# Inverse roots of the queries' and keys' mean squares by GpSimd, projections earlier in the order, in the first stage of a two-layer transformer kernel

## The reference

```
def _rmsnorm(x, scale):
    ms = jnp.mean(jnp.square(x), axis=-1, keepdims=True)
    return x * jax.lax.rsqrt(ms + EPS) * scale
...
h = _layernorm(x) * (1 + ca) + sa
q = (xh @ wq + bq).reshape(b, s, 16, 16)
k = (xh @ wk + bk).reshape(b, s, 4, 16)
v = (xh @ wv + bv).reshape(b, s, 4, 16)
q = _rmsnorm(q, q_norm_scale)
k = _rmsnorm(k, k_norm_scale)
q, k = rope(q) * head_scale, rope(k)
probs = softmax(causal(q k^T * head_scale))
x = x + ga * (probs v @ wo + bo)
h = _layernorm(x) * (1 + cb) + sb
x = x + gb * ffn(h)
```

## Time and profile before

| | |
|---|---|
| median of 3 runs | 1146.43 us (1146.34 to 1146.93) |
| profiled execution | 1145.18 us, of which the span of instructions is 1143.5 us |
| mean granted TensorE clock | 0.970 |
| first stage | from 0 to about 241 us of the span |
| later stages | attention of the second layer to about 965 us, then the experts |

### The profile page before, as it was taken

The page is one execution under the profiler, slowest core; times in us unless marked ns, Lnnn a source line. Parts: engine busy times, 40 slices in busy tenths (PEclk is TensorE's granted clock), DMA queues, the critical chain, the costliest instruction groups (busy, mean ns, idle before and its releaser), DMA issues. The chain is left out here.

```text
span 1143.5 us, 22333 instructions
## 1 busy us (share of the span) xinstructions
PE 1060.2 (93%) x7536; PEld 923.7 (81%) x7536; DVE 895.2 (78%) x1817; ACT 736.2 (64%) x1399; POOL 334.6 (29%) x335
## 2 busy tenths in 40 slices
PE   5888888879999999999999999999999997979996
PEld 4656666658899899899898898898998986769994
DVE  5788988857788788788788788788788787867775
ACT  4679797767766666666666666666666654625661
POOL 3353544442311201211111111111111234753440
PEclk9889999979999999999999999999999998989999
DMA  7210001010401311311311211221221291824436
GB/s 256 94 52 16 16 6 44 14 50 23 137 21 50 112 47 47 108 45 52 100 51 53 94 58 53 89 62 53 80 71 54 83 45 66 355 98 116 123 98 234
DMA packets 67881, 92.13 MB, mean 81 GB/s; under 512 B 22658, under 2 KB 46338, under 8 KB 66787
## 3 DMA queue, kind: packets, MB, share of 16 engines
q1 hardware_dynamic: 64402, 81.83, 24.6%
q0 software_dynamic: 3408, 9.39, 2.2%
HBM read 46.35 MB, written 42.75 MB: 78 GB/s over the span
## 5 line engine op out<-in xcount | busy, mean ns | idle before, releaser
L1551 PE MATMUL all_psum<-all_h_parts,attn_wp 128*128 128x512 f32 x1140 | 297.6, 396 | 0.0
L1551 PEld LDWEIGHTS all_psum<-all_h_parts,attn_wp 128*128 128x128 f32 x1140 | 209.8, 189 | 39.7
L1723 ACT CAST attn_pp<-attn_p 128x512 fp32r<-128x512 f32 (+3 forms) x256 | 117.4, 459 | 187.8 <-DVE attn_p L1831 185.7
L1812 DVE TENSOR_TENSOR attn_pp<-attn_p,attn_pp 128x512 fp32r<-128x512 f32 (+3 forms) x256 | 198.0, 773 | 6.5 <-ACT attn_pp L1723 6.5
L1970 POOL TENSOR_TENSOR all_gate<-all_gate,attn_sq 128x512 f32<-128x512 f32 x64 | 84.7, 1324 | 369.8 <-ACT attn_sq L1734 369.7
L1630 PE MATMUL all_psum<-attn_qkp 128*128 128x512 f32 (+3 forms) x768 | 164.9, 323 | 3.7 <-DVE attn_qkp L1812 3.7
L1577 PE MATMUL all_psum<-attn_pp,attn_vp 128*128 128x512 f32 (+3 forms) x768 | 163.8, 322 | 1.0 <-DVE attn_pp L1812 0.5
L1577 PEld LDWEIGHTS all_psum<-attn_pp,attn_vp 128*128 128x128 f32 x768 | 129.4, 189 | 21.6 <-issue 1.2
L1630 PEld LDWEIGHTS all_psum<-attn_qkp 128*128 128x128 f32 x768 | 124.8, 190 | 12.6 <-issue 4.3
L1831 DVE TENSOR_TENSOR attn_p<-all_psum,attn_mask 128x512 f32<-128x512 f32 (+3 forms) x256 | 123.5, 482 | 2.1 <-PE all_psum L1630 0.9
L1054 DVE TENSOR_REDUCE front_top<-all_psum 128x2 f32<-128x256 f32 (+3 forms) x128 | 99.4, 815 | 17.8 <-PE all_psum L695 16.8
(11 more groups left out here) (381 smaller groups left out, 1899.5 us busy)
## 6 DMA issues: line engine op xcount, KB each, us to landing
expert_rows<-attn_empty SPq DMA_DIRECT2D x8, 2080.0 KB, 12.7
expert_weight_parts<-all_wraw SPq DMA_DIRECT2D x32, 304.0 KB, 2.4
experts_wx<-expert_weight_parts SPq DMA_DIRECT2D x8, 1216.0 KB, 16.6
all_wraw<-in_w1p SPq DMA_DIRECT2D x8, 1024.0 KB, 5.9
all_yacc<-expert_rows SPq DMA_DIRECT2D x39, 130.5 KB
all_wraw<-in_wx SPq DMA_DIRECT2D x16, 304.0 KB, 3.0
attn_mask<-decay_masks SPq DMA_DIRECT2D x16, 256.0 KB, 2.6
all_x<-in_x SPq DMA_DIRECT2D x4, 512.0 KB, 7.0
```

What stands on the lines that cost most here:

```text
L1551: last = nc.tensor.matmul(out, wp[:, a, k, col:col + P], hh[:, c, k, b * S:(b + 1) * S], start=(m == 0), stop=(m == 5))
L1723: nc.scalar.copy(pp[:, u % 2, 0, cols], p[:, cols]).then_inc(p_hi, 1)
L1812: nc.vector.tensor_tensor(out, whole, high.bitcast(F32), ALU.subtract).then_inc(ready, 1)
```

## The change

The mean and the root of batches 1 to 3 go from ACT and DVE to POOL: a tensor_scalar (times 1/16, plus EPS) and a tensor_tensor with the operation pow and the exponent -0.5, each on 128x80. ACT's Sqrt and DVE's reciprocal remain for batch 0 alone. In the prologue's table, L norm, xt, pj0, pj1, sq, ss and std come earlier by 4 to 9 and more events, rms and qn later by 2 to 5, and krot, which stood ahead of rms, now stands behind qn.

```
-PROLOGUE_AT = {"L stats": (0, 0), "L rstd": (0, 0), "L norm": (0, 10), "xt": (0, 13), "pj0": (0, 17), "pj1": (0, 17),
-               "sq": (1, 1), "ss": (1, 9), "std": (1, 12), "krot": (1, 13), "rms": (1, 14), "qn": (1, 18),
-               "rot": (2, 0), "va": (2, 8), "rope": (2, 11), "kt": (2, 12), "qt0": (2, 17)}
+PROLOGUE_AT = {"L stats": (0, 0), "L rstd": (0, 0), "L norm": (0, 5), "xt": (0, 8), "pj0": (0, 11), "pj1": (0, 13),
+               "sq": (0, 17), "ss": (1, 4), "std": (1, 5), "rms": (1, 19), "qn": (1, 20),
+               "krot": (1, 20), "rot": (2, 1), "va": (2, 8), "rope": (2, 11), "kt": (2, 12), "qt0": (2, 17)}
...
                     elif kind == "std":
-                        b = ev[1]
+                        if ev[1]:
+                            continue
                         act.wait_ge(eps_set, 1)
-                        act.wait_ge(ss_done, b + 1)
+                        act.wait_ge(ss_done, 1)
...
-                    elif kind == "rms":
-                        dve.wait_ge(std_done, ev[1] + 1)
+                    elif ev == ("rms", 0):
+                        dve.wait_ge(std_done, 1)
                         nc.vector.reciprocal(ss[:, :, :], ss[:, :, :]).then_inc(rrms_done, 1)
...
+                    elif kind == "std" and ev[1]:
+                        b = ev[1]
+                        pool.wait_ge(ss_done, b + 1)
+                        nc.gpsimd.tensor_scalar(ss[:, :, :], ss[:, :, :], 1.0 / D0, EPS_RMS, ALU.mult, ALU.add
+                                                ).then_inc(mean_done, 1)
+                        pool.wait_ge(mean_done, b)
+                        nc.gpsimd.tensor_tensor(ss[:, :, :], ss[:, :, :],
+                                                t["neg_half"][:, 0:1].unsqueeze(2).to_broadcast([P, TB, NH]), ALU.pow
+                                                ).then_inc(rrms_done, 1)
```

More of the change, by code:

```diff
@@ L521, in front_stage @@
         w_scaled, w_high, w_ready = n.sem("w_scaled"), n.sem("w_high"), n.sem("w_ready")
+        mean_done = n.sem("mean_done")
         qkv_done, v_copied, sq_done, ss_done, std_done, rrms_done = (
```

## The result

The changed kernel takes 1196.7 us (median of 4 runs, 1194.66 to 1198.93) against 1146.68 us beside it: ratio 1.0441, 95% interval 1.0427 to 1.0456. It is 50 us slower. The forecast of 1179 named the direction and lies within its range of 1152 to 1200, but it is 18 us short. The profiled execution took 1194.66 us, with a span of 1192.9.

The account below looks back on a forecast made before the run. DVE was taken to bound g5 and g6. Later qn starts of 9.1, 12.6 and 12.6 us made 34.3, less 2: 1177.5 us profiled, 1179 for the time; range 1152 to 1200.

Parts of the forecast that it names:

- The bound: In g5 and g6 of the first stage, DVE is busy 12.99 of 13.90 and 12.35 of 12.60 us, so DVE's waits count.
- The bound of 4.7 us on what goes away: Removing ACT's root and table loads and DVE's reciprocal wins at most 1.6 us per batch, 4.7 us for three.
- The power: POOL's pow on 128x80 takes 12.3 us, from the line through 4 and 8 elements; ends of range 1.2 and 20.9.
- The rival of a short power: First rival listed: pow costs 1.2 us, only the reordering is left, +13.5 us, time 1160; chance 0.09.
- The wait for "out": In g4, pj0 ahead in PE's queue waits for xt's scaling, so DVE has "out" at 102.5 instead of 98.08.
- so sq does come earlier: Batch 1 has no post work, so its squares start earlier; ss was put at 61.5 us.
- qn's start: qn starts later than before by 9.1 us in batch 1 and 12.6 us each in batches 2 and 3.
- they bring DVE to qn at about 120.4: In batch 2, six score maxima behind ss take 5.6 us; DVE then idles until qn starts at 127.1.
- Behind each qn, DVE is the bound for the next 12 us, so nothing is caught up there: After qn, DVE is busy 12.35 of 12.60 us, so the delay at qn isn't recovered there.
- the 2 us taken off for g7: In g7 and its like, where ACT has less in arrears, 2 us come back: 34.3 becomes 32.3.

Follow-up runs that it names:

- the order alone: Changed kernel's table of moved entries, with the old root on ScalarE and VectorE at its old places, against the kernel before: 1175.46 us, ratio 1.0271.
- The projections alone: Kernel before with only L norm, xt, pj0 and pj1 at their new earlier places: 1157.87 us, ratio 1.0114.
- the product experiment: Changed kernel with a product in place of the power, inverse root left out: 1169.93 us, ratio 1.0225 against the kernel before.
- the pair without the power: Kernel before with sq earlier, qn, krot, rot later, ss and root at old places: 1153.95 us; the same with A low and bias behind krot: 1146.10 us.

## Why the forecast had the sign right and the size 18 us short

**The bound: right.** DVE was the engine to watch in g5 and g6. The bound of 4.7 us on what goes away held as a size: with the product in place of the root it came to 5.5 us against the order alone, a little over the bound and within the noise of it. In the changed kernel it doesn't show, since DVE waits for the power in the place where it would be won.

**The power: right in kind, 6% short.** The line through 4 and 8 elements gave 12.3 us, the runs 13.1. Three times 0.8 makes 2.4 us of the gap. The Trainium skill's "GPSIMD Engine Reference", section "Elementwise — side-by-side cycle accounting", has one price, measured on an addition, and by it the power would have taken about as long as the product, 0.32 us here; for the product the price fits, for pow the measurement (0.16 us per element) decides against it. The rival of a short power was wrong as to the power, and its 1160 was 10 us short as to the order (1169.93 measured).

**The wait for "out": right to a tenth.** I had it 4.4 us late in g4; it was 114.94 against 98.08 with g4 beginning 12.5 us late, so 4.4. That sq doesn't come earlier in batches 2 and 3 was right too: DVE waited 3.06 us before ss where I had 2.6. The projections alone confirm the mechanism. In batch 1 the forecast was wrong about the squares ("so sq does come earlier"): they began at 56.61 against 55.85, since g0, too, stood for the norm, and the next group began 3.5 us late where the sum had 2.4.

**qn's start: 1 to 2 us short per batch.** Net of the batches before, qn started 11.2, 13.7 and 14.4 us late, where the sum had 9.1, 12.6 and 12.6. The power is 0.8 of it each time. The rest came ahead of the power: ss ended 1.5, 0.4 and 1.1 us later than laid out (in batch 3 "out" was 5.2 us late), less 0.2 for the mean and its hops, which I had too dear. The step "they bring DVE to qn at about 120.4" was short by 3 us: the last maxima of g5 were late by themselves, 2.07 and 1.11 us behind PE, and DVE was ready for qn at 135.9, 123.4 without the 12.5 lost before. That moved nothing here, for DVE still had 4.75 us to wait. It counts where there is no power: in the product experiment qn was 3.1, 7.5 and 10.0 us late, where the first rival had 1.7, 5.9 and 5.9.

**The failed step: "Behind each qn, DVE is the bound for the next 12 us, so nothing is caught up there", and the 2 us taken off for g7.** It assumed that nothing is added either. Between qn and the end of the batch the loss grew by 0.9, 4.2 and 5.6 us, 10.6 in all, where I took off 2. I had listed A low, bias and krot behind the power and asked only whether they would be done in time, not what ran beside them. In the kernel before they ran after qn and its rotation (A low started at 120.39 there, the second product ended at 118.9); held up to the end of the power they fell on qn and the second product, +2.1 and +1.6 us in batches 2 and 3 on the engine that is the bound. Moving them behind krot took 7.3 us of that growth away again, and the pair without the power shows the same in the time (1153.95 to 1146.10). What remains, 3 to 4 us, isn't a matter of the new order: with the power alone in the old table, the loss behind qn grows by 0.8, 0.6 and 1.7 us as well. What makes it was not taken apart. A suspect is TensorE's clock. In g6 its granted clock had a mean of 0.72 where the earlier trace rows have 1.00, and in this window PE had stood still for 10.27 us:

```profile
137.70:161.70 24.00, 12.27 (x115) 8.94 (x112) 19.11 (x20) 6.84 (x13) 16.28 (x10) 0.72 0.02 5
```

```profile
149.73 0.48 PE L703 MATMUL all_psum<-front_qt,front_kt 128*128 128x384 f16 x1 [10.27 <-DVE front_top L1056]
```

The first is the window of g6 in the changed kernel, columns as in the earlier trace rows: 24.0 us long, where it was 12.6. But the clock was nearly as low in g6 with A low and bias moved (0.77) and with the power alone (0.79), where behind qn only 0.8 and 0.6 us were added. So it isn't the clock that made the 4.2; whether it has a part in what remains stays open, since no experiment changed it alone.

**The account**, by the q2 copies. Short by 18: 2.4 for the power's length, 2.6 for the other delays up to qn (most of it the later ss), 12.6 behind qn (10.6 and the 2 taken off), and 0.4 at the start.

## What to carry to other kernels

Before giving an operation to an idle engine, read its price per element from two sizes in the trace, and hold that against the slack of the one instruction that waits for it; a share of 29% busy says nothing about a 13 us latency in a chain that had 4 us between the sum and its use. In queues that are served in order, an event that is moved forward takes its own wait with it and hands it to all behind it: the projections, put ahead of a norm that wasn't ready, cost 13 us and bought no earlier squares in any batch; in batches 2 and 3 GpSimd's queue had another wait ahead of them. And ask of everything that queues up behind a long instruction not only when it is done, but what will run beside it when it is let go.

## What the runs showed of the hardware that I had not expected

GpSimd's and VectorE's instructions with two SBUF inputs didn't share the time, they took turns. A low ran its usual 2.34 us from 140.62, and qn, started at 140.68, took 3.62: A low's end at 142.96 and then 1.34 more, near the 1.48 that it takes alone. The product of 128x256 behind A low then waited for qn in turn, 1.97 us instead of 0.73. Whoever came first kept the way. The Trainium skill, "Advanced Engine Details and Errata", section "GPSIMD Details", says that GpSimd shares a read and a write interface with VectorE and conflicts with VectorE's instructions that have two SBUF inputs; the traces agree, and here the later of the two waited for the other's end. The power doesn't hold that way for its 13.1 us: inside it, at 68.75, VectorE's two-input product of 128x16 took its usual 0.23 us, and so it did inside every power that it met in four of the kernels, ten in all. Beside an ordinary two-input instruction it is held up: in the kernel before, the same product of 128x16 took 1.35 us at 129.35, beside the A add of 128.27. The power of 128x80 took 13.10 or 13.11 us in every batch of the three kernels that have it.
